# Four batches of normalised attention on one core: group statistics batch by batch, and the small step behind each row maximum on another engine

## The chip, the core and the metric

The kernel runs on one core of a Trainium2 chip. The metric is the device time of one execution in microseconds (us), taken as the median of several runs. The engines are named as in the profile: PE (TensorE, matrix products), PEld (its weight loads), DVE (VectorE), ACT (ScalarE), POOL (GpSimd) and SP (the queue that issues most transfers). They run their own instruction streams in order and wait for each other by semaphores.

## The reference

The input x has 4 batches of 128 channels and 32 x 32 = 1024 positions, all in float32. What is computed, for each batch:

```python
# 4 groups of 32 channels; mean and variance over a group's channels and all positions
y = (xg - mu) * rsqrt(var + 1e-5)
y = y * gamma + beta
q, k, v = split(w_qkv @ y + b_qkv)
w = softmax(q^T k * 128 ** -0.5)      # 1024 x 1024
out = x + w_out @ (v w^T) + b_out
```

## The kernel before

**Folding.** The products of the weight matrices are made once at the start. Scores come from z = (folded Wq, Wk) y and y itself, so a batch needs y, z and the values v (with the output matrix already in them). Most matrices are held as a head and a tail (names in _hi and _lo), and each product of them is three matmuls: hi by hi, hi by lo, lo by hi.

**Tiling.** A batch has 8 blocks of 128 query rows (i = 0 to 7), and each block has 1024 keys. "Block (b, i)" is block i of batch b. The steps of a block are:
- PE: scores of the block into PSUM, 128 x 1024 (block_scores, L601 to L604).
- DVE: negated row maximum (maximum, L427), then a small 128 x 1 operation that makes `shift` out of the maximum and the key bias of the row (L435).
- ACT: exponential with `shift` as bias, and the row sums (L276).
- DVE: reciprocal of the row sums, inv_sum (L440).
- POOL: probabilities times inv_sum (normalise, L216). "Normalisation" below is this.
- PE: eight 128 x 128 transposes (turn, L614), in two halves j = 0, 1.
- ACT and DVE: head and tail of the turned halves (pt_hi L285, pt_lo L447).
- PE: mixing with the values (mix, L634 to L636), a quarter of a half-batch at a time. The result of a half-batch is made on DVE (L454) and stored by SP.

**Order.** Every engine has its order written out by hand in a loop over b and i. In pass (b, i) PE makes the scores two blocks ahead, (b, i + 2), then turns block (b, i), then does a job of the next batch, then mixes. DVE takes the maximum of block i + 2, the tails of block i, a tail of a job, the result if one is due, then inv_sum of block i + 2. ACT makes the heads of block i and the exponential of block i + 2. POOL normalises block i + 2. Batch 0 has no mixing in its passes 0 to 3, since there is nothing to mix yet.

**Jobs of the next batch.** They project z in two halves (Z0, Z1) and the values in three parts (V0, V1, V2) into one PSUM bank, `projected`. JOB_SLOT puts Z0, V0, V1, Z1 into passes 4, 5, 6, 7 of the batch before; V2 comes in pass 0 of the batch itself. Each job waits until DVE has taken the tail of the one before (s_pj_lo, L567).

**Normalising x into y.** For batch 0 it is done in pieces at the start. For batch 1, POOL makes y in pass (0, 0) (L246) and its tail in passes (0, 2) and (0, 3) (y_tail, L211). For batches 2 and 3, DVE makes y in pass (b, 1) (L390), ACT its head in pass (b, 2), and POOL its tail in pass (b, 3) of the batch before.

**Statistics.** DVE: bn_stats of each half of x (L354, 128 x 512), bn_aggr to mean and variance of a channel (L359). PE: the deviation of each channel's mean from its group's, and the negated group mean (group_means, L547 and L549). DVE: spread (L367). PE: group variance (group_variances, L554). DVE: variance + eps (L372). POOL: power -0.5 (rstd_of, L204). DVE: norm_a, norm_b (coefficients, L378, L381). Batches 2 and 3 are done together: their four bn_stats stand in DVE's passes (0, 4) to (0, 7), group_means at the end of PE's pass (1, 0) behind a wait for the tail of V2 (L724), group_variances at the end of pass (1, 1), and the DVE and POOL steps in pass (1, 1).

Of the kernel before, what the change touches and what calls it, by code (L numbers as in the profile page):

```python
# [5 lines left out]
def attention_kernel(nc, x, vectors, weights, out):  # L6
# [4 lines left out]
    ALU = mybir.AluOpType  # L11
# [29 lines left out]
    with ctx:  # L41
# [33 lines left out]
        spread = sb("spread", [C, BATCHES])  # L75
        var_eps = sb("var_eps", [C, BATCHES])
        rstd = sb("rstd", [C, BATCHES])
        norm_a = sb("norm_a", [C, BATCHES])
        norm_b = sb("norm_b", [C, BATCHES])

# [18 lines left out]
        mixed = ps("mixed", [C, HALF])  # L99
        projected = ps("projected", [128, HALF])  # L100

        DEV, MINUS_MEAN, VARIANCE = 0, 8, 16
        setup = scores[:, 1, :]
        SET_W, SET_V, SET_OUT, SET_U, SET_S, SET_Z, SET_G = 0, 256, 384, 385, 386, 387, 512

# [8 lines left out]
        s_spread = sem("channel_spreads_ready")  # L114
        s_gvar = sem("group_variances_ready")
        s_var_eps = sem("variance_eps_ready")
        s_rstd = sem("rstd_ready")
        s_norm = sem("norm_ready")
        s_bias_product = sem("bias_product_ready")
# [66 lines left out]
        @block_ctx.gpsimd  # L186
        def _(pool):
            pool.memset(ident[:, :], 0.0).then_inc(s_const, 1)
            pool.memset(group_mean[:, :], 0.0).then_inc(s_const, 1)
            pool.memset(minus_half[:, :], -0.5).then_inc(s_const, 1)  # L190
            pool.memset(ones[:, :], 1.0).then_inc(s_const, 1)
            pool.wait_ge(s_const, 4)
            pool.affine_select(out=ident[:, :], in_=ident[:, :], compare_op=ALU.not_equal, fill=1.0,
                               base=0, pattern=[[-1, 128]], channel_multiplier=1).then_inc(s_const, 1)
            for g in range(GROUPS):
                pool.wait_ge(s_const, 5 + g)
                pool.memset(group_mean[g * CG:(g + 1) * CG, g * CG:(g + 1) * CG], 1.0 / CG).then_inc(s_const, 1)
            pool.wait_ge(s_const, 5 + GROUPS)
            pool.tensor_tensor(centring[:, :], ident[:, :], group_mean[:, :], ALU.subtract).then_inc(s_const, 1)
            pool.tensor_scalar(minus_mean[:, :], group_mean[:, :], -1.0, None, ALU.mult).then_inc(s_const, 1)  # L200

            def rstd_of(lo, hi, n):
                pool.wait_ge(s_var_eps, n)
                pool.tensor_tensor(rstd[:, lo:hi], var_eps[:, lo:hi], minus_half[:, lo:hi],  # L204
                                   ALU.pow).then_inc(s_rstd, 1)

            def y_tail(b, h):
                half = slice(h * HALF, (h + 1) * HALF)
                pool.wait_ge(s_y, b)
                pool.wait_ge(s_y_hi, b)  # L210
                pool.tensor_tensor(y_lo[:, b % 2, half], y[:, b % 2, half], y_hi[:, b % 2, half].bitcast(fp32),  # L211
                                   ALU.subtract).then_inc(s_y_lo, 1)

            def normalise(b, i):
                pool.wait_ge(s_inv, BLOCKS * b + i + 1)
                pool.tensor_scalar(probs[:, i % RING, :], probs[:, i % RING, :], inv_sum[:, i:i + 1], 1.0,  # L216
                                   ALU.mult, ALU.mult).then_inc(s_probs, 1)

            pool.wait_ge(s_vecs, 16)
            pool.tensor_tensor(bias_product[:, :], BQ, BK, ALU.mult).then_inc(s_bias_product, 1)  # L220
            rstd_of(0, 1, 1)
            rest = slice(SPLIT, N)
            pool.wait_ge(s_norm, 1)
            pool.tensor_scalar(y[:, 0, rest], xs[:, 0, rest], norm_a[:, 0:1], norm_b[:, 0:1],
                               ALU.mult, ALU.add).then_inc(s_y0_rest, 1)
            pool.wait_ge(s_y0_rest, 1)
            pool.wait_ge(s_y0_hi, 3)
            pool.tensor_tensor(y_lo[:, 0, rest], y[:, 0, rest], y_hi[:, 0, rest].bitcast(fp32),
                               ALU.subtract).then_inc(s_y0_lo_rest, 1)
            normalise(0, 0)  # L230
            rstd_of(1, 2, 2)
            normalise(0, 1)
            for b in range(BATCHES):
                for i in range(BLOCKS):
                    behind = 0 < b < BATCHES - 1 and i == 3
                    if behind:
                        y_tail(b + 1, 0)
                    if after(b, i, 2)[0] < BATCHES:
                        normalise(*after(b, i, 2))
                    if behind:  # L240
                        y_tail(b + 1, 1)
                    if b == 1 and i == 1:
                        rstd_of(2, BATCHES, 3)
                    if b == 0 and i == 0:
                        pool.wait_ge(s_norm, 2)
                        pool.tensor_scalar(y[:, 1, :], xs[:, 1, :], norm_a[:, 1:2], norm_b[:, 1:2],  # L246
                                           ALU.mult, ALU.add).then_inc(s_y, 1)
                    if b == 0 and i in (2, 3):
                        y_tail(1, i - 2)
# [95 lines left out]
        def _(dve):  # L345
# [29 lines left out]
            def coefficients(lo, hi, n, minus_means):  # L375
                dve.wait_ge(s_rstd, n)
                dve.wait_ge(s_gmean, 2 * n)
                step(dve.tensor_scalar(norm_a[:, lo:hi], rstd[:, lo:hi], GAMMA, None, ALU.mult))  # L378
                dve.wait_ge(s_step, steps_done[0])
                for b in range(lo, hi):  # L380
                    dve.scalar_tensor_tensor(out=norm_b[:, b:b + 1],  # L381
                                             in0=minus_means[:, MINUS_MEAN + b:MINUS_MEAN + b + 1],
                                             scalar=norm_a[:, b:b + 1], in1=BETA, op0=ALU.mult,
                                             op1=ALU.add).then_inc(s_norm, 1)

# [21 lines left out]
            def projection_tail(b, job):  # L407
                dve.wait_ge(s_pj_hi, job_count(b, job))
                if job in V_TILES:
                    key_biases(b, job, projected)  # L410
                    value_tails(b, job, projected, s_pj_lo)
                else:
                    half = slice(0, HALF) if job == Z0 else slice(HALF, N)
# [10 lines left out]
            def maximum(b, i):  # L424
                n = BLOCKS * b + i
                dve.wait_ge(s_scores, n + 1)
                dve.tensor_reduce(neg_max[:, i:i + 1], scores[:, i % 2, :], AX.X, ALU.max,  # L427
                                  negate=True).then_inc(s_max, 1)
                bias = key_bias[:, b % 2, i:i + 1]
                if n == 0:  # L430
                    dve.wait_ge(s_setup, 5)
                    first_key_biases(V0, turned[:, 1, :])
                dve.wait_ge(s_key_bias, 3 * b + min(i // 3, 2) + 1)
                dve.wait_ge(s_max, n + 1)
                dve.tensor_scalar(shift[:, i:i + 1], neg_max[:, i:i + 1], bias, bias, ALU.subtract,  # L435
                                  ALU.add).then_inc(s_shift, 1)

            def inverse_sum(b, i):
                dve.wait_ge(s_exp, BLOCKS * b + i + 1)
# [23 lines left out]
            variances(0, 1, 1, projected)  # L463
            half_stats(1, 0)
            dve.wait_ge(s_vecs, 16)
            coefficients(0, 1, 1, mixed)

            dve.wait_ge(s_norm, 1)
            pieces = (slice(0, FIRST), slice(FIRST, SPLIT))
# [35 lines left out]
            first_value_tails(V0, turned[:, 1, :])  # L505
            inverse_sum(0, 1)
            first_z_tail(3, projected[:, :], HALF, N)
            coefficients(1, 2, 2, mixed)

            for b in range(BATCHES):  # L510
                last = b + 1 == BATCHES
                for i in range(BLOCKS):
# [6 lines left out]
                    if b == 0 and i in (0, 1):  # L519
                        first_key_biases((V1, V2)[i], (mixed, projected)[i])  # L520
                        first_value_tails((V1, V2)[i], (mixed, projected)[i])
                    if b == 1 and i == 1:
                        channel_spreads(2, BATCHES, 6, projected)
                    if i in JOB_SLOT and not last:
                        projection_tail(b + 1, JOB_SLOT[i])
                    if i == 7:
# [2 lines left out]
                        results(b - 1, 1, mixed)  # L529
                    if ahead[0] < BATCHES:  # L530
                        inverse_sum(*ahead)
                    if b == 0 and i >= QB:
                        half_stats(2 + (i - QB) // 2, i % 2)
                        if i == 7:
                            channel_stats(2, BATCHES)
                    if b == 1 and i == 1:
                        variances(2, BATCHES, 3, projected)
                        coefficients(2, BATCHES, 3, projected)
                    if 0 < b and i == 1 and not last:
                        normalised(b + 1)  # L540
            results(BATCHES - 1, 1, projected)
# [2 lines left out]
        def _(pe):  # L544
# [17 lines left out]
                return mm  # L562

            def projection(b, job):
                if b == 2 and job == Z0:
                    pe.wait_ge(s_norm, BATCHES)
                if job_count(b, job) > 1:  # L567
                    pe.wait_ge(s_pj_lo, job_count(b, job) - 1)
                if job in V_TILES:
                    pe.wait_ge(s_y, b)  # L570
                    if b == 1 and job == V0:
                        pe.wait_ge(s_v0_lo, 3)
                    mm = values(b, job, projected)
                else:
                    half = slice(0, HALF) if job == Z0 else slice(HALF, N)
# [124 lines left out]
            for b in range(BATCHES):  # L700
                last = b + 1 == BATCHES
                for i in range(BLOCKS):
# [17 lines left out]
                        mix(b, 0, i - QB, mixed)  # L720
                    elif b > 0:
                        mix(b - 1, 1, i, mixed)
                    if b == 1 and i == 0:
                        pe.wait_ge(s_pj_lo, job_count(1, V2))  # L724
                        group_means(2, BATCHES, projected, projected)
                    if b == 1 and i == 1:
                        group_variances(2, BATCHES, projected)
            for chunk in range(QB):
                mix(BATCHES - 1, 1, chunk, projected)

# [30 lines left out]
```

## Time and profile before

| what | value |
|---|---|
| median of 3 runs | 153.50 us (153.49 to 153.58) |
| the profiled execution's own time | 153.87 us |
| its span (first to last instruction) | 152.1 us |
| PE busy | 143.5 us, 94% of the span |
| DVE busy | 117.5 us, 77% |
| ACT busy | 89.2 us, 59% |
| POOL busy | 51.3 us, 34% |
| granted PE clock | 1.00 |

The profile is of one execution. Its time is 1.77 us more than its span, and 0.37 us above the median of the runs. Times in the rows count from the start of the span. In a timeline row, the first number is the start of a group of instructions and the second the time from there to its end; where an instruction follows another on DVE or PE without a wait, it starts a little before the end of the first, since they are pipelined, so start-to-start distances are what an instruction costs its engine.

### The profile page before, as it was taken

The numbers are of one execution on the slowest core, as the hardware profiler recorded it, in microseconds if no ns is written. First come the engines' busy times: TensorE is split into PE (matmuls) and PEld (weight loads), VectorE is DVE, ScalarE is ACT, GpSimd is POOL, SyncE is SP. The second block draws the span as 40 slices with busy tenths as digits, with TensorE's granted clock in tenths as the row PEclk, the third lists the DMA queues.
The fourth block names the chain that finished last, engine by engine and source line by source line (L and its number), as shares of the span: only waits on it lengthen the run. The fifth ranks groups of instructions, "written<-read, shape, count | busy, mean of one in ns | idle before, by whom it ended". The sixth has DMA issues, their size and how long they took to land.

```text
span 152.1 us, 2244 instructions
## 1 busy us (share of the span) xinstructions
PE 143.5 (94%) x791; PEld 118.3 (78%) x791; DVE 117.5 (77%) x235; ACT 89.2 (59%) x163; POOL 51.3 (34%) x60
## 2 busy tenths in 40 slices
PE   7999999889999698999999999999999999999991
PEld 7977686578888577788888888888888888887880
DVE  0697799999889755997788979797779777977501
ACT  3164787896555543676677656866555666667200
POOL 6131517582222214176212224662221323232000
PEclk9999999999999999999999999999999999999999
DMA  5930000000000100001000200010000100010011
GB/s 176 312 134 0 0 4 0 2 0 0 4 2 18 51 0 0 0 23 50 0 0 0 73 0 2 0 71 0 4 0 3 66 0 0 10 66 0 0 69 69
DMA packets 2316, 4.60 MB, mean 30 GB/s; under 512 B 385, under 2 KB 385, under 8 KB 2305
## 3 DMA queue, kind: packets, MB, share of 16 engines
q1 hardware_dynamic: 2016, 4.20, 7.8%
q10 hardware_dynamic: 288, 0.27, 0.5%
q8 instruction: 6, 0.10, 0.3%
q14 instruction: 6, 0.04, 0.1%
HBM read 2.36 MB, written 2.10 MB: 29 GB/s over the span
## 4 chain that ended last, share of the span: by engine, by line
PE 80%; DVE 15%; ACT 2%; issue 1%; DVEq 0%
PE turned L614 15%; PE scores L601 8%; PE mixed L636 8%; PE scores L604 8%; PE mixed L635 8%; PE scores L602 8%; PE mixed L634 8%; DVE neg_max L427 5%; DVE pt_lo L447 4%; PE scores L641 4%; PE projected L560 3%; ACT probs L276 2%; DVE shift L435 1%; PE projected L636 1%; PE projected L635 1%
## 5 line engine op out<-in xcount | busy, mean ns | idle before, releaser
L216 POOL TENSOR_SCALAR probs<-probs,inv_sum 128x1024 f32<-128x1024 f32 x32 | 36.4, 1138 | 82.1 <-DVE inv_sum L440 82.1
L285 ACT ACTIVATE pt_hi<-turned 128x512 fp32r<-128x512 f32 x64 | 34.9, 595 | 39.1 <-PE turned L614 39.0
L427 DVE TENSOR_REDUCE neg_max<-scores 128x1 f32<-128x1024 f32 x32 | 39.0, 1218 | 12.8 <-PE scores L604 12.2
L447 DVE TENSOR_TENSOR pt_lo<-turned,pt_hi 128x512 fp32r<-128x512 f32 x64 | 40.9, 681 | 1.7 <-ACT pt_hi L285 1.7
L276 ACT ACTIVATE probs<-scores,shift 128x1024 f32<-128x1024 f32 x32 | 35.7, 1115 | 4.8 <-DVE shift L435 3.7
L614 PEld LDWEIGHTS turned<-ident,probs 128*128 128x128 f32 x256 | 29.3, 140 | 8.7 <-issue 3.5
L614 PE MATMUL turned<-ident,probs 128*128 128x128 f32 x256 | 34.0, 275 | 1.9 <-DVE pt_lo L447 1.5
L601 PE MATMUL scores<-y_hi,z_hi 128*128 128x512 f32 x62 | 24.9, 402 | 0.0
L602 PE MATMUL scores<-y_lo,z_hi 128*128 128x512 f32 x62 | 24.5, 395 | 0.0
L634 PE MATMUL mixed<-pt_hi,v_hi 128*128 128x512 f32 x56 | 23.9, 427 | 0.0
L636 PE MATMUL mixed<-pt_hi,v_lo 128*128 128x512 f32 x56 | 22.1, 395 | 0.0
L635 PE MATMUL mixed<-pt_lo,v_hi 128*128 128x512 f32 x56 | 22.1, 394 | 0.0
L604 PE MATMUL scores<-y_hi,z_lo 128*128 128x512 f32 x62 | 19.4, 394 | 0.0
L601 PEld LDWEIGHTS scores<-y_hi,z_hi 128*128 128x128 f32 x62 | 11.7, 188 | 2.7 <-issue 0.4
L604 PEld LDWEIGHTS scores<-y_hi,z_lo 128*128 128x128 f32 x62 | 11.6, 188 | 2.7
L602 PEld LDWEIGHTS scores<-y_lo,z_hi 128*128 128x128 f32 x62 | 11.7, 188 | 2.5
L636 PEld LDWEIGHTS mixed<-pt_hi,v_lo 128*128 128x128 f32 x56 | 10.5, 187 | 2.5
L635 PEld LDWEIGHTS mixed<-pt_lo,v_hi 128*128 128x128 f32 x56 | 10.6, 189 | 1.6
L634 PEld LDWEIGHTS mixed<-pt_hi,v_hi 128*128 128x128 f32 x56 | 10.6, 189 | 1.6
L435 DVE TENSOR_SCALAR shift<-neg_max,key_bias 128x1 f32<-128x1 f32 x32 | 8.7, 273 | 3.4
L211 POOL TENSOR_TENSOR y_lo<-y,y_hi 128x512 fp32r<-128x512 f32 x6 | 7.8, 1296 | 0.0
L354 DVE BATCH_NORM_STATS2 stats<-xs 128x6 f32<-128x512 f32 x8 | 5.4, 680 | 2.9 <-DMA xs<-in_x_dram 2.9
(142 smaller groups left out, 139.8 us busy)
## 6 DMA issues: line engine op xcount, KB each, us to landing
out_dram<-result SPq DMA_DIRECT2D x8, 256.0 KB, 2.1
xs<-in_x_dram SPq DMA_DIRECT2D x2, 512.0 KB, 6.7
xs<-in_x_dram SPq DMA_DIRECT2D x3, 256.0 KB, 4.6
xs<-in_x_dram ACTq DMA_DIRECT2D x1, 256.0 KB, 3.3
ws<-in_weights_dram SPq DMA_DIRECT2D x1, 256.0 KB, 4.4
vecs<-in_vectors_dram ACTq DMA_DIRECT2D x1, 3.0 KB, 4.6
```

Source lines behind the costliest of these rows:

```text
L216: pool.tensor_scalar(probs[:, i % RING, :], probs[:, i % RING, :], inv_sum[:, i:i + 1], 1.0, ALU.mult, ALU.mult).then_inc(s_probs, 1)
L276: act.activation(probs[:, i % RING, :], scores[:, i % 2, :], ACT.Exp, bias=shift[:, i:i + 1], accum_out=row_sum[:, i:i + 1]).then_inc(s_ex ...
L285: act.activation(pt_hi[:, g, j * 4:(j + 1) * 4, i % QB * 128:(i % QB + 1) * 128], turned[:, j, :].rearrange("p (k n) -> p k n", n=128), AC ...
L427: dve.tensor_reduce(neg_max[:, i:i + 1], scores[:, i % 2, :], AX.X, ALU.max, negate=True).then_inc(s_max, 1)
L447: dve.tensor_tensor(pt_lo[to], turned[:, j, :].rearrange("p (k n) -> p k n", n=128), pt_hi[to].bitcast(fp32), ALU.subtract).then_inc(s_pt_ ...
L601: pe.matmul(to[h], z_hi[:, b % 2, query], y_hi[:, b % 2, halves[h]], start=True, stop=False)
L602: pe.matmul(to[h], z_hi[:, b % 2, query], y_lo[:, b % 2, halves[h]], start=False, stop=False)
L604: mm = pe.matmul(to[h], z_lo[:, b % 2, query], y_hi[:, b % 2, halves[h]], start=False, stop=True)
L614: mm = pe.transpose(turned[:, j, k * 128:(k + 1) * 128], probs[:, i % RING, key:key + 128], ident[:, :])
L634: pe.matmul(bank[:, :], v_hi[v], pt_hi[:, g, k, :], start=(k == 0), stop=False)
L635: pe.matmul(bank[:, :], v_hi[v], pt_lo[:, g, k, :], start=False, stop=False)
L636: mm = pe.matmul(bank[:, :], v_lo[v], pt_hi[:, g, k, :], start=False, stop=(k == KT - 1))
```

## The change

Two edits, made together.

1. The operation that makes `shift` leaves DVE's stream (behind each maximum) and is issued by POOL instead. In pass (b, i) POOL makes `shift` of block i + 2 first, before its normalisation of the same block; the y and y_lo operations that POOL has in batch 0 stay behind the normalisation of their pass, and so stand in front of the next pass's `shift`. For blocks (0, 0) and (0, 1) POOL makes both shifts before the first normalisation.
2. The statistics of batches 2 and 3 are separate. Batch 2's bn_stats stand in DVE's passes (0, 4), (0, 5), batch 3's in (1, 4), (1, 5). group_means of batch b + 1 is issued just before the values of job V1 of batch b, group_variances just before those of job V2, in the same PSUM bank beyond the columns of the values (columns 400, 408, 416). DVE makes spread and a copy of the negated mean inside the tail of V1, and variance + eps inside that of V2. POOL makes rstd in pass (b, 0) behind the normalisation. The two waits at the end of PE's passes (1, 0) and (1, 1), and the wait before Z0 of batch 2, are gone.

```diff
-        DEV, MINUS_MEAN, VARIANCE = 0, 8, 16
+        DEV, MINUS_MEAN, VARIANCE = 400, 408, 416
...
@@ POOL
+            def shifts(b, i):
+                n = BLOCKS * b + i
+                bias = key_bias[:, b % 2, i:i + 1]
+                pool.wait_ge(s_key_bias, 3 * b + min(i // 3, 2) + 1)
+                pool.wait_ge(s_max, n + 1)
+                pool.tensor_scalar(shift[:, i:i + 1], neg_max[:, i:i + 1], bias, bias, ALU.subtract,
+                                   ALU.add).then_inc(s_shift, 1)
...
+            shifts(0, 0)
+            shifts(0, 1)
             normalise(0, 0)
             rstd_of(1, 2, 2)
             normalise(0, 1)
             for b in range(BATCHES):
                 for i in range(BLOCKS):
+                    if after(b, i, 2)[0] < BATCHES:
+                        shifts(*after(b, i, 2))
                     behind = 0 < b < BATCHES - 1 and i == 3
                     if behind:
                         y_tail(b + 1, 0)
...
-                    if b == 1 and i == 1:
-                        rstd_of(2, BATCHES, 3)
+                    if 0 < b < BATCHES - 1 and i == 0:
+                        rstd_of(b + 1, b + 2, b + 2)
@@ DVE, projection_tail
                     key_biases(b, job, projected)
+                    if job == V1 and b + 1 < BATCHES:
+                        channel_spreads(b + 1, b + 2, 2 * (b + 2), projected)
+                        dve.tensor_copy(negated_mean[:, b + 1:b + 2],
+                                        projected[:, MINUS_MEAN + b + 1:MINUS_MEAN + b + 2]).then_inc(s_negated, 1)
+                    if job == V2 and b + 1 < BATCHES:
+                        variances(b + 1, b + 2, b + 2, projected)
                     value_tails(b, job, projected, s_pj_lo)
@@ DVE, maximum
-                dve.wait_ge(s_key_bias, 3 * b + min(i // 3, 2) + 1)
-                dve.wait_ge(s_max, n + 1)
-                dve.tensor_scalar(shift[:, i:i + 1], neg_max[:, i:i + 1], bias, bias, ALU.subtract,
-                                  ALU.add).then_inc(s_shift, 1)
@@ DVE, loop
-                    if b == 1 and i == 1:
-                        channel_spreads(2, BATCHES, 6, projected)
...
-                    if b == 0 and i >= QB:
-                        half_stats(2 + (i - QB) // 2, i % 2)
-                        if i == 7:
-                            channel_stats(2, BATCHES)
-                    if b == 1 and i == 1:
-                        variances(2, BATCHES, 3, projected)
-                        coefficients(2, BATCHES, 3, projected)
+                    if b + 2 < BATCHES and i in (4, 5):
+                        half_stats(b + 2, i - 4)
+                        if i == 5:
+                            channel_stats(b + 2, b + 3)
+                    if 0 < b < BATCHES - 1 and i == 1:
+                        dve.wait_ge(s_negated, b)
+                        coefficients(b + 1, b + 2, b + 2, negated_mean[:, b + 1:b + 2])
@@ PE, projection
-                if b == 2 and job == Z0:
-                    pe.wait_ge(s_norm, BATCHES)
...
+                    if job == V1 and b + 1 < BATCHES:
+                        group_means(b + 1, b + 2, projected, projected)
+                    if job == V2 and b + 1 < BATCHES:
+                        group_variances(b + 1, b + 2, projected)
                     mm = values(b, job, projected)
@@ PE, loop
-                    if b == 1 and i == 0:
-                        pe.wait_ge(s_pj_lo, job_count(1, V2))
-                        group_means(2, BATCHES, projected, projected)
-                    if b == 1 and i == 1:
-                        group_variances(2, BATCHES, projected)
```

## Rows read from the trace of the kernel before

**Rows 1.** The page, part 1: busy time, share of the span and instructions.

```profile
PE 143.5 (94%) x791; PEld 118.3 (78%) x791; DVE 117.5 (77%) x235; ACT 89.2 (59%) x163; POOL 51.3 (34%) x60
```

**Rows 2.** Windows of PE alone: stretch, length, busy (instructions), clock, DMA, GB/s.

```profile
51.14:53.00 1.86, 0.64 (x6) 1.00 0.00 0
...
56.74:58.03 1.29, 0.41 (x3) 1.00 0.00 0
58.03:137.85 79.82, 79.82 (x445) 1.00 0.05 18
```

**Rows 3.** Timeline of PE: start, length, instruction, idle before and its releaser.

```profile
52.53 0.38 PE L547 MATMUL projected<-mean_var,centring 128*128 128x2 f32 x2 [1.22 <-DVE v_lo L404]
...
57.79 0.38 PE L554 MATMUL projected<-spread,group_mean 128*128 128x2 f32 x2 [0.88 <-DVE spread L367]
```

**Rows 4.** Timeline of DVE: passes (0, 0), (0, 1), and the end of (0, 5).

```profile
19.04 1.21 DVE L427 TENSOR_REDUCE neg_max<-scores 128x1 f32<-128x1024 f32 x1
...
20.55 1.28 DVE L447 TENSOR_TENSOR pt_lo<-turned,pt_hi 128x512 fp32r<-128x512 f32 x2
...
22.34 0.15 DVE L440 RECIPROCAL inv_sum<-row_sum 128x1 f32<-128x1 f32 x1
22.41 1.20 DVE L427 TENSOR_REDUCE neg_max<-scores 128x1 f32<-128x1024 f32 x1
...
38.90 0.15 DVE L440 RECIPROCAL inv_sum<-row_sum 128x1 f32<-128x1 f32 x1
38.97 0.67 DVE L354 BATCH_NORM_STATS2 stats<-xs 128x6 f32<-128x512 f32 x1
```

**Rows 5.** Timeline of POOL: passes (0, 0) and (0, 2).

```profile
22.58 1.12 POOL L216 TENSOR_SCALAR probs<-probs,inv_sum 128x1024 f32<-128x1024 f32 x1 [3.07 <-DVE inv_sum L440]
23.69 1.19 POOL L246 TENSOR_SCALAR y<-xs,norm_a,norm_b 128x1024 f32<-128x1024 f32 x1
...
29.85 1.29 POOL L211 TENSOR_TENSOR y_lo<-y,y_hi 128x512 fp32r<-128x512 f32 x1
```

**Rows 6.** Chain that ended last, pass (0, 2): from shift to inv_sum.

```profile
26.95 0.28 DVE shift L435
...
27.25 1.22 ACT probs L276 x2
```

**Rows 7.** Groups of instructions of POOL by form: busy, mean ns of one, idle before.

```profile
L246 POOL TENSOR_SCALAR y<-xs,norm_a,norm_b 128x1024 f32<-128x1024 f32 x1 | 1.2, 1193 | 0.0
L204 POOL TENSOR_TENSOR rstd<-var_eps,minus_half 128x1 f32<-128x1 f32 x2 | 1.1, 563 | 1.2 <-DVE var_eps L372 1.2
...
L224 POOL TENSOR_SCALAR y<-xs,norm_a,norm_b 128x384 f32<-128x384 f32 x1 | 0.7, 721 | 0.7 <-DVE norm_b L381 0.7
L204 POOL TENSOR_TENSOR rstd<-var_eps,minus_half 128x2 f32<-128x2 f32 x1 | 0.7, 712 | 0.0
L200 POOL TENSOR_SCALAR minus_mean<-group_mean 128x128 f32<-128x128 f32 x1 | 0.5, 535 | 0.0
...
L220 POOL TENSOR_TENSOR bias_product<-vecs 128x1 f32<-128x1 f32 x1 | 0.2, 194 | 2.3 <-DMA vecs<-in_vectors_dram 2.3
```

**Rows 8.** Timeline of PE: group_means of batch 1, and job V1 in pass (0, 6).

```profile
12.28 0.28 PE L547 MATMUL mixed<-mean_var,centring 128*128 128x1 f32 x2
...
12.64 0.92 PE L560 MATMUL turned<-wv_out,y 128*128 128x129 f32 x6
...
40.59 0.83 PE L560 MATMUL projected<-wv_out,y 128*128 128x129 f32 x6
```

**Rows 9.** Timeline of PE: turned blocks (1, 2) and (3, 6), then (3, 7).

```profile
63.32 1.17 PE L614 MATMUL turned<-ident,probs 128*128 128x128 f32 x8
...
138.36 1.16 PE L614 MATMUL turned<-ident,probs 128*128 128x128 f32 x8
...
140.77 1.04 PE L614 MATMUL turned<-ident,probs 128*128 128x128 f32 x8
```

**Rows 10.** Waits: who waited for whom, us in total, times, longest.

```profile
DVE neg_max L427 <- PE scores L604: 12.2, 17, 2.1
```

More of the change, by code:

```diff
@@ L77, in attention_kernel @@
         rstd = sb("rstd", [C, BATCHES])
+        negated_mean = sb("negated_mean", [C, BATCHES])
         norm_a = sb("norm_a", [C, BATCHES])
@@ L116, in attention_kernel @@
         s_var_eps = sem("variance_eps_ready")
+        s_negated = sem("negated_mean_kept")
         s_rstd = sem("rstd_ready")
@@ L380, in coefficients @@
                 for b in range(lo, hi):
-                    dve.scalar_tensor_tensor(out=norm_b[:, b:b + 1],
-                                             in0=minus_means[:, MINUS_MEAN + b:MINUS_MEAN + b + 1],
+                    dve.scalar_tensor_tensor(out=norm_b[:, b:b + 1], in0=minus_means[:, b - lo:b - lo + 1],
                                              scalar=norm_a[:, b:b + 1], in1=BETA, op0=ALU.mult,
@@ L428, in maximum @@
                                   negate=True).then_inc(s_max, 1)
-                bias = key_bias[:, b % 2, i:i + 1]
                 if n == 0:
@@ L465, in _ @@
             dve.wait_ge(s_vecs, 16)
-            coefficients(0, 1, 1, mixed)
+            coefficients(0, 1, 1, mixed[:, MINUS_MEAN:MINUS_MEAN + 1])
             dve.wait_ge(s_norm, 1)
@@ L507, in _ @@
             first_z_tail(3, projected[:, :], HALF, N)
-            coefficients(1, 2, 2, mixed)
+            coefficients(1, 2, 2, mixed[:, MINUS_MEAN + 1:MINUS_MEAN + 2])
             for b in range(BATCHES):
```

## The prediction

> **What bounds the kernel now.** Read the busy shares first: PE has 94% of the span, its clock is granted in full, and DVE has 77% [rows 1]. So only what keeps PE waiting, or gives it more to do, can move the end. I then cut PE's timeline into windows at its waits. From 58.03 to 137.85 us it is busy without a break [rows 2]: nothing taken off DVE, ACT or POOL there is worth anything while the rest still arrives in time. The waits stand earlier. (a) In passes (0, 0) to (0, 3), where nothing is mixed, PE follows DVE, and the chain of waits runs through maximum, shift, tails and inv_sum. (b) From 51.14 to 53.00 and from 56.74 to 58.03 PE stands before, and then does, the statistics matmuls of batches 2 and 3 [rows 2]; the releasers are DVE's v_lo and spread [rows 3]. Everything after 58.03 follows these two without slack, up to the last result.
>
> **Statistics: what goes.** With the waits gone, PE would go on with the next scores at 51.14 and 56.74. So 1.86 + 1.29 = 3.15 us leave the path, of which the matmuls are 0.47 (52.53 to 53.00) and 0.24 (57.79 to 58.03) [rows 2, 3]. What is late next? The scores of block (1, 3) need only the exponential of (1, 1), and the turn behind them needs DVE's tail of block (1, 0), which loses two bn_stats and two bn_aggr ahead of it (0.67 each, and less for the others) as well as a shift. I expect no new wait there.
>
> **What comes.** Per batch, group_means with one column costs PE 12.64 - 12.28 = 0.36 [rows 8] and group_variances about 0.25, taken at the 0.24 of the two-column one [rows 3]. Twice that, all on PE's path: 1.22. DVE gets two copies, one more variance, one more norm_a, each near 0.2, and bn_stats of batch 3 in passes (1, 4) and (1, 5). I cost these at nothing: DVE waits for PE's scores 17 times, 12.2 us in all [rows 10]. Without that cover they would be 0.8 and 1.6. POOL's rstd moves one pass ahead, behind normalisation (b, 2), and is wanted only after DVE's maximum and tails of the next pass. No DMA moves; the removed wait before Z0 of batch 2 held nothing.
>
> **Shift: what DVE saves.** From maximum to tails DVE needs 20.55 - 19.04 = 1.51 [rows 4]. A maximum with no dependent behind it holds DVE 1.14 (its 1.21, less the 0.07 by which 22.41 follows 22.34 + 0.15 = 22.49). So 0.37 less per block. In the PE-bound stretch that is worth nothing, except where DVE's tail held back the second half of a turn: blocks (1, 2) and (3, 6) take 1.17 and 1.16 where an unhindered one takes 1.04, and each also began late, about 0.27 in all for each [rows 9]. These go: 0.54.
>
> **Shift: what the new place costs.** The trace has no 128 x 1 POOL operation with two pointer operands. The y operations have that form: 1193 ns for 1024 columns, 721 for 384, so 0.74 ns a column and 0.44 us for none; the 128-column one of 535 ns lies on the same line [rows 7]. Bounds: 0.19 us, the one-column product, below; 0.71, the two-column power, above [rows 7]. I take s = 0.44, by the rows of the same operation. [...]
>
> The longer step alone would be hidden. What counts is POOL's order. Shift of the next block stands behind y (1.19) in pass (0, 0) and behind y_lo (1.29) in passes (0, 2) and (0, 3), and these start 1.11 after their normalisation [rows 5]. The chain in batch 0, from one inv_sum to the next, is then as follows.
> - inv_sum to normalisation 0.24 (22.34 to 22.58), to y 1.11, y 1.16: shift starts 2.51 after inv_sum [rows 4, 5]. Then s, 0.04 to ACT, 1.24 from exponential to inv_sum (27.25, with 1.22) [rows 6]: 3.79 + s = 4.23.
> - Behind y_lo: 0.10 more, 4.33.
> - With a free POOL: 0.07 to the maximum, 1.21, 0.09 to POOL, then the same: 2.65 + s = 3.09.
>
> Start: the maximum of (0, 2) at 19.04 [rows 4], moved by 0.07 for the shift before it. Shift 20.41, exponential 20.89, inv_sum (0, 2) at 22.13 (before, 22.34). Then (0, 3) behind y, 26.36; (0, 4), 29.45; (0, 5) behind y_lo, 33.78; (0, 6) behind y_lo, 38.11. DVE goes on: 0.07 and 0.60 for bn_stats, maximum 1.14, then the 1.79 that lie between 20.55 and 22.34 [rows 4] for tails, key_bias and v_lo: inv_sum (0, 7) at 41.71, where it was at 38.90 [rows 4]. Behind it come bn_stats (0.07 later, 0.67 [rows 4]) and a bn_aggr, for which I estimate 0.24, as for any small operation behind a wait on DVE; together 0.98, and only then may PE begin group_means, at about 42.8. It began V1 at 40.59 [rows 8]. So PE loses 2.2 us in batch 0; part of it is lost by pass (0, 4) already. The edits meet here: with either alone PE would not stand behind both POOL's queue and the new statistics. Behind that point the passes are mixed ones, longer than the chain, and no y work is on POOL.
>
> In batches 1 and 2 y_lo holds up the shift of block 6 too, by some 1.4 us. Its cover is the two-block lead: by the same steps bn_aggr of batch 3 ends about 0.5 us before PE wants it in pass (1, 6). I cost it at nothing.
>
> **Sum**, against the profiled execution: 153.87 - 3.15 - 0.54 + 1.22 + 2.2 = 153.6. The median of the runs stands 0.37 below that execution, so 153.2 is my forecast for it.
>
> **Rivals.**
> 1. The small operation is cheap (0.19). Five of them lie in the chain (blocks 2 to 6), one of them limited by DVE: 1.2 less, 152.0. For it: the product [rows 7]. Against it: the line of the y rows.
> 2. Slower: it is dear, as the power is (0.56 for one column, 0.71 for two [rows 7]), or takes as much longer to be noticed by ACT. Place: the same five steps in front of group_means in pass (0, 6). Five times 0.12 gives 153.8, five times 0.27 gives 154.5. It decides from about 0.50 on, where the whole gain is used up.
> 3. POOL's order doesn't bite: PE reaches V1 as before, because the exponentials have slack that I don't see. Then 153.50 - 3.15 - 0.54 + 1.22 = 151.0. Against it: the chain of waits runs through shift in these passes. What DVE saves there can't show, since inv_sum waits for the exponential.
> 4. The statistics of batch 3 come too late in pass (1, 6): each 0.1 beyond the 0.5 of cover costs 0.1, some 0.5 in all with the forecast's other terms, 153.7.
>
> **Chances.** Forecast 0.42, rival 1 0.20, rival 2 0.20, rival 3 0.08, rival 4 0.10. The range 151.9 to 154.4 leaves out rival 3 and the far end of rival 2. No change is within 0.2%, 0.3 us, about what a measurement of this kernel can tell. The forecast lies at its edge: I split it 0.22 faster, 0.15 same, 0.05 slower. Rivals 1 and 3 add 0.28 to faster, rivals 2 and 4 give 0.22 to slower and 0.08 to same. Faster 0.50, same 0.23, slower 0.27.
>
> **What would show it.** Right: shift of POOL near 440 ns; that of block (0, 3) starting right behind y, those of (0, 5) and (0, 6) right behind y_lo; inv_sum (0, 6) near 38; PE idle before group_means at about 41.5 to 42.8; the stretches of 1.86 and 1.29 gone; PE without a break from there on. Wrong: shift far from 440 ns, no idle time of PE before group_means in pass (0, 6), or a new wait of PE after 45 us.

## The result, and the profile after

The changed kernel takes 154.62 us (median of 6 runs, 154.37 to 154.87), the kernel before 153.53 (median of 6, 153.44 to 153.79): a ratio of 1.0069, 95% interval 1.0056 to 1.0083. It is slower; the forecast was 153.2 us and a range up to 154.4. Ratios here leave out a run that stands more than 1.5% above the fastest of its kernel: one of 6 of the kernel with POOL's order below (154.34) and one of 12 of the changed kernel with the other norm_b (156.63).

| what | before | after |
|---|---|---|
| the profiled execution's own time | 153.87 us | 154.79 us |
| its span | 152.1 us | 153.0 us |
| PE busy | 143.5 us | 144.6 us |
| DVE busy | 117.5 us | 112.2 us |
| POOL busy | 51.3 us | 62.7 us |

The page of the changed kernel, parts 1 and 5, against [rows 1] and [rows 7] (an engine's busy time; then line, operation, count, busy us, mean ns, idle before it and its releaser):

```profile
PE 144.6 (95%) x797; PEld 120.0 (78%) x797; DVE 112.2 (73%) x207; ACT 89.0 (58%) x163; POOL 62.7 (41%) x93
...
L226 POOL TENSOR_SCALAR shift<-neg_max,key_bias 128x1 f32<-128x1 f32 x32 | 11.7, 366 | 25.1 <-DVE neg_max L446 22.2
```

DVE has 5.3 us less to do, POOL 11.4 us more; the 32 shifts are 11.7. Neither is the bound. What counts is which of them PE waits for. POOL's timeline after, from pass (0, 0) to pass (0, 4), answers to [rows 5]:

```profile
22.86 1.13 POOL L218 TENSOR_SCALAR probs<-probs,inv_sum 128x1024 f32<-128x1024 f32 x1 [1.54 <-DVE inv_sum L454]
23.97 1.19 POOL L260 TENSOR_SCALAR y<-xs,norm_a,norm_b 128x1024 f32<-128x1024 f32 x1
25.15 0.36 POOL L226 TENSOR_SCALAR shift<-neg_max,key_bias 128x1 f32<-128x1 f32 x1
27.04 1.12 POOL L218 TENSOR_SCALAR probs<-probs,inv_sum 128x1024 f32<-128x1024 f32 x1 [1.53 <-DVE inv_sum L454]
28.23 0.36 POOL L226 TENSOR_SCALAR shift<-neg_max,key_bias 128x1 f32<-128x1 f32 x1
30.13 1.12 POOL L218 TENSOR_SCALAR probs<-probs,inv_sum 128x1024 f32<-128x1024 f32 x1 [1.53 <-DVE inv_sum L454]
31.22 1.27 POOL L213 TENSOR_TENSOR y_lo<-y,y_hi 128x512 fp32r<-128x512 f32 x1
32.48 0.37 POOL L226 TENSOR_SCALAR shift<-neg_max,key_bias 128x1 f32<-128x1 f32 x1
34.38 1.11 POOL L218 TENSOR_SCALAR probs<-probs,inv_sum 128x1024 f32<-128x1024 f32 x1 [1.53 <-DVE inv_sum L454]
35.46 1.29 POOL L213 TENSOR_TENSOR y_lo<-y,y_hi 128x512 fp32r<-128x512 f32 x1
36.73 0.37 POOL L226 TENSOR_SCALAR shift<-neg_max,key_bias 128x1 f32<-128x1 f32 x1
```

Three of these four shifts stand behind a normalisation and y or y_lo, the one at 28.23 behind a normalisation alone; after each shift POOL idles 1.53 us. DVE's timeline of the changed kernel shows who waits for the exponential behind that shift, and where the statistics of batch 2 end, against [rows 4]:

```profile
26.78 0.16 DVE L454 RECIPROCAL inv_sum<-row_sum 128x1 f32<-128x1 f32 x1 [1.24 <-ACT probs L290]
...
34.12 0.16 DVE L454 RECIPROCAL inv_sum<-row_sum 128x1 f32<-128x1 f32 x1 [1.53 <-ACT probs L290]
...
38.37 0.16 DVE L454 RECIPROCAL inv_sum<-row_sum 128x1 f32<-128x1 f32 x1 [1.11 <-ACT probs L290]
...
42.06 0.16 DVE L454 RECIPROCAL inv_sum<-row_sum 128x1 f32<-128x1 f32 x1
...
42.84 0.21 DVE L373 BATCH_NORM_AGGREGATE mean_var<-stats 128x2 f32<-128x12 f32 x1
```

DVE stands still for 1.24, 1.53 and 1.11 us. PE's timeline of the changed kernel, from the turn in pass (0, 6) on, against [rows 8] (V1 began at 40.59):

```profile
40.99 1.16 PE L628 MATMUL turned<-ident,probs 128*128 128x128 f32 x8
43.20 0.35 PE L559 MATMUL projected<-mean_var,centring 128*128 128x1 f32 x2 [1.04 <-DVE mean_var L373]
43.42 0.36 PE L561 MATMUL projected<-mean_var,minus_mean 128*128 128x1 f32 x2
43.64 0.92 PE L572 MATMUL projected<-wv_out,y 128*128 128x129 f32 x6
```

**Where the time went.** The turns (eight transposes a block, one group in PE's timeline) serve as milestones. In both kernels all up to group_means of batch 1 on PE is the same, and it came 0.45 later in the changed kernel's trace (12.73, before 12.28 [rows 8]); that is taken off here. Distances are after minus before.

| PE begins | after - before, less 0.45 | what happened since the row above |
|---|---|---|
| turn (0, 4) | +0.78 | shift of block (0, 3) behind y |
| turn (0, 6) | +0.82 | shift of block (0, 5) behind y_lo, covered by mixing |
| turn (0, 7) | +2.68 | PE waits for bn_aggr of batch 2, then group_means |
| turn (1, 1) | +0.95 | the old wait of 1.86 is gone |
| turn (1, 2) | -0.41 | the old wait of 1.29 is gone |
| turn (1, 3) | -0.20 | held back itself, for pt_lo of block (1, 2) |
| turn (1, 7) | +0.39 | group_means of batch 3, and a short wait |
| turn (2, 1) | +0.60 | group_variances of batch 3 |
| turn (2, 4) | +0.74 | turn (2, 3) held back, for pt_lo of block (2, 2) |
| turn (3, 6) | +0.44 | nothing holds it back any more |
| last result | +0.48 | |

One name has to be put right first. The row at 63.32 in [rows 9] is the turn of block (1, 3), not (1, 2) as its heading and the prediction say, and some expectations below repeat it: it waits for pt_lo of block (1, 2). In the changed kernel the same turn has a wait that PE's timeline shows:

```profile
63.57 1.16 PE L628 MATMUL turned<-ident,probs 128*128 128x128 f32 x8 [0.21 <-DVE pt_lo L461]
```

From group_means of batch 1 to the last result the kernel before takes 136.57 us (12.28 to 148.85) and the changed one 137.05 (12.73 to 149.78). I call this the body; its end is the start of the last result on DVE. A second trace of the kernel before gave the same 136.57, and no other kernel was traced twice: two traces that agree are the ground for comparing bodies to a few hundredths, more closely than the medians.

### The profile page after: what moved, and what is told of

Same layout as the page of the kernel before. It is cut to its first block, busy times and chain, and to the rows that moved or that the text cites. A ratio compares the mean times of both kernels' runs of the same rounds, so it can differ in the third digit from the quotient of the medians.

```text
span 153.0 us, 2261 instructions
## 1 busy us (share of the span) xinstructions
PE 144.6 (95%) x797; PEld 120.0 (78%) x797; DVE 112.2 (73%) x207; ACT 89.0 (58%) x163; POOL 62.7 (41%) x93
## 4 chain that ended last, share of the span: by engine, by line
PE 74%; DVE 10%; POOL 6%; ACT 4%; issue 3%; POOLq 0%
PE turned L628 14%; PE mixed L650 7%; PE mixed L648 7%; PE mixed L649 7%; PE scores L616 7%; PE scores L618 7%; PE scores L615 7%; DVE neg_max L446 5%; ACT probs L290 4%; PE scores L655 4%; PE projected L572 3%; POOL probs L218 2%; POOL shift L226 2%; POOL y_lo L213 2%; PE projected L650 1%
## 5 line engine op out<-in xcount | busy, mean ns | idle before, releaser
L218 POOL TENSOR_SCALAR probs<-probs,inv_sum 128x1024 f32<-128x1024 f32 x32 | 35.8, 1119 | 46.4 <-DVE inv_sum L454 46.4
L226 POOL TENSOR_SCALAR shift<-neg_max,key_bias 128x1 f32<-128x1 f32 x32 | 11.7, 366 | 25.1 <-DVE neg_max L446 22.2
L454 DVE RECIPROCAL inv_sum<-row_sum 128x1 f32<-128x1 f32 x32 | 5.2, 162 | 14.0 <-ACT probs L290 13.4
L572 PE MATMUL projected<-wv_out,y 128*128 128x129 f32 x52 | 7.8, 281 | 0.0
```

## Experiments

**The kernel before, traced again.** No edit.

> The kernel before once more, for a second trace of it. Expected: 153.5 us, the 1.86 and 1.29 us waits again. Open: whether the first matmuls behind the warm-up run at the short or the long spacing, and where the profiled execution of 153.87 us lost 0.37 us against the median.

Measured: 153.62 us, span 151.8, body 136.57, batch 1's group_means at 12.03. The waits stand as before. So the 0.37 us of the first trace don't lie in the body; 0.25 of them lie ahead of 12.28.

**Each edit alone.** First the statistics, with shift in DVE's stream again:

```diff
@@ POOL, shifts
                 n = BLOCKS * b + i
+                if not (False):
+                    return
...
@@ DVE, maximum
+                if True:
+                    bias = key_bias[:, b % 2, i:i + 1]
+                    dve.wait_ge(s_key_bias, 3 * b + min(i // 3, 2) + 1)
+                    dve.wait_ge(s_max, n + 1)
+                    dve.tensor_scalar(shift[:, i:i + 1], neg_max[:, i:i + 1], bias, bias, ALU.subtract,
+                                      ALU.add).then_inc(s_shift, 1)
```

> Edit 2 alone; shift is made by DVE again. Theory (the statistics pay 1.9 us, the place of shift in POOL's order takes them back): the waits of 1.86 and 1.29 us are gone, 1.2 us of small matmuls come, PE doesn't wait before group_means in pass (0, 6); 151.6 to 151.9 us. Rival (the statistics matmuls inside the value jobs are what costs): 153.5 us or more, with PE idle before group_means in pass (0, 6).

Measured: 152.15 us, ratio 0.9887 (0.9867 to 0.9906), body 135.05, 1.52 less than before. bn_aggr of batch 2 is done well ahead of PE:

```profile
39.81 0.21 DVE L375 BATCH_NORM_AGGREGATE mean_var<-stats 128x2 f32<-128x12 f32 x1
```

```profile
40.73 0.28 PE L567 MATMUL projected<-mean_var,centring 128*128 128x1 f32 x2
40.87 0.36 PE L569 MATMUL projected<-mean_var,minus_mean 128*128 128x1 f32 x2
41.09 0.92 PE L580 MATMUL projected<-wv_out,y 128*128 128x129 f32 x6
```

The first fence is DVE's timeline, the second PE's, both of this kernel: no releaser stands behind L567. The expected 151.6 to 151.9 was missed by 0.25, for which the run with the other norm_b, below, has the cause. Then shift on POOL in the kernel before, with the statistics untouched (shifts as in the change, and DVE's own operation gone):

```diff
...
+            shifts(0, 0)
+            shifts(0, 1)
             normalise(0, 0)
...
+                    if after(b, i, 2)[0] < BATCHES:
+                        shifts(*after(b, i, 2))
...
```

> Edit 1 alone; the statistics of batches 2 and 3 as before. Theory: inv_sum of blocks (0, 3), (0, 5), (0, 6) late as in the changed kernel, PE 1.2 us late by pass (0, 4) and more by pass (0, 6), where it waits for v_lo; the two old waits stand but are shorter, as DVE has less to do: 153.7 to 154.8 us. Rival (the move of shift is free, the two edits only collide at group_means): within 0.3 us of 153.5.

Measured: 154.09 us beside 154.10 of the kernel before in the same runs, 1.0013 (0.9996 to 1.0029); the time decides nothing, the trace does. inv_sum of (0, 3), (0, 5), (0, 6) came late behind y and y_lo, and PE was 1.19 us late at turn (0, 7) and 0.42 in the body. PE's waits in this kernel (us in total, times, longest), against the 1.22 and 0.88 of [rows 3]:

```profile
PE projected L554 <- DVE v_lo L416: 1.0, 1, 1.0
...
PE projected L561 <- DVE spread L379: 0.5, 1, 0.5
```

So the move of shift costs 1.2 us in batch 0 and is paid back in part by the two old waits, which shrink since DVE has less to do. Together with edit 2 nothing is left to shrink, and a new wait stands in front of group_means. The parts don't add: -1.52 and +0.42 alone, +0.48 together.

**POOL's order.** Both edits, but y and the y_lo operations stand behind the shift of the next pass and ahead of its normalisation:

```diff
                     if after(b, i, 2)[0] < BATCHES:
                         shifts(*after(b, i, 2))
-                    behind = 0 < b < BATCHES - 1 and i == 3
-                    if behind:
-                        y_tail(b + 1, 0)
-                    if after(b, i, 2)[0] < BATCHES:
-                        normalise(*after(b, i, 2))
-                    if behind:
-                        y_tail(b + 1, 1)
-                    if 0 < b < BATCHES - 1 and i == 0:
-                        rstd_of(b + 1, b + 2, b + 2)
-                    if b == 0 and i == 0:
+                    if b == 0 and i == 1:
                         pool.wait_ge(s_norm, 2)
                         pool.tensor_scalar(y[:, 1, :], xs[:, 1, :], norm_a[:, 1:2], norm_b[:, 1:2],
                                            ALU.mult, ALU.add).then_inc(s_y, 1)
-                    if b == 0 and i in (2, 3):
-                        y_tail(1, i - 2)
+                    if b == 0 and i in (3, 4):
+                        y_tail(1, i - 3)
+                    if 0 < b < BATCHES - 1 and i in (3, 4):
+                        y_tail(b + 1, i - 3)
+                    if after(b, i, 2)[0] < BATCHES:
+                        normalise(*after(b, i, 2))
+                    if 0 < b < BATCHES - 1 and i == 0:
+                        rstd_of(b + 1, b + 2, b + 2)
```

> Both edits, but POOL's y and y_lo operations stand behind the next block's shift and ahead of its normalisation, where POOL was idle. Theory (the order of POOL's queue): shifts start within 0.2 us of their maximum, inv_sum (0, 6) before 36.5, no wait of PE before group_means in pass (0, 6) beyond 0.3 us: 151.6 to 152.4 us. Rival (the longer operation and the second handover by themselves): PE's loss in batch 0 remains at 1.5 us or more, above 153.5 us.

Measured: 151.87 us, ratio 0.9853 (0.9827 to 0.988), body 134.42, 2.63 less than the changed kernel's. POOL's timeline in this kernel:

```profile
22.97 1.13 POOL L218 TENSOR_SCALAR probs<-probs,inv_sum 128x1024 f32<-128x1024 f32 x1 [1.53 <-DVE inv_sum L451]
24.17 0.36 POOL L226 TENSOR_SCALAR shift<-neg_max,key_bias 128x1 f32<-128x1 f32 x1
24.51 1.19 POOL L251 TENSOR_SCALAR y<-xs,norm_a,norm_b 128x1024 f32<-128x1024 f32 x1
26.07 1.12 POOL L218 TENSOR_SCALAR probs<-probs,inv_sum 128x1024 f32<-128x1024 f32 x1 [0.36 <-DVE inv_sum L451]
```

y now lies in the 1.53 us in which POOL had been idle, and delays nobody: inv_sum (0, 6) starts at 35.11, bn_aggr at 39.81. The instructions, their lengths and the handover are the same as in the changed kernel, so the rival (the longer operation by itself) falls.

**Only y moved.** As above for y alone; the y_lo operations stay.

> The changed kernel with only y of batch 1 moved behind the shift of block (0, 3); the y_lo operations stay where the change has them. Theory (each of the three y operations delays the chain by its own length): inv_sum (0, 3) 1.1 us earlier, PE at group_means 1.1 us earlier, 153.4 to 153.6 us. Rival (y_lo are enough to make PE late, y is hidden): 154.3 us or more.

Measured: 153.27 us, ratio 0.9966 (0.9946 to 0.9986), body 136.07, 0.98 less than the changed kernel's. From batch 1's group_means to those of batch 2 it takes 29.44 (12.34 to 41.78), in the changed kernel 30.47 (12.73 to 43.20) and with all three operations moved 28.05 (12.82 to 40.87). So of 2.42, y alone makes 1.03 and the y_lo operations the rest. The time is 0.13 below the expected range, the 1.1 expected at group_means was 1.03.

**A second shift.** A useless copy in front of each of five shifts of batch 0:

```diff
+                if 2 <= n <= 6:
+                    pool.tensor_scalar(spare[:, i:i + 1], neg_max[:, i:i + 1], bias, bias, ALU.subtract,
+                                       ALU.add)
```

> The changed kernel with a second, useless copy of the shift operation on POOL in front of each of the shifts of blocks 2 to 6 of batch 0 (it writes a spare tile). Theory (all five lie in the chain in front of group_means in pass (0, 6)): five times about 0.35, group_means 1.6 to 1.8 us later than in the changed kernel, 156.2 to 156.4 us. Rival (only those behind y and y_lo are in the chain): three times 0.35, 155.6 us. If nothing is in the chain: 154.6.

Measured: 155.90 us, ratio 1.0135 (1.0111 to 1.016), body 138.55. Counted from batch 1's group_means (12.09 here), those of batch 2 start at 32.25, in the changed kernel at 43.20 - 12.73 = 30.47: 1.78 later, five times 0.36. All five stand in the chain: it is this distance that decides against the rival of three, since the time lies between the two forecasts. The body is 1.50 longer: 0.3 is given back where turn (1, 3) is held up less. The time came out 0.3 below the expected range.

**Shift on DVE in batch 0 only.** The changed kernel with the shifts of b = 0 in DVE's stream.

> The changed kernel with shift on DVE in batch 0 and on POOL in batches 1 to 3. Theory (only the five shifts of batch 0 in front of group_means are late on PE's path): 151.9 to 152.3 us, near edit 2 alone. Rival (shift on POOL costs in every batch): halfway, 153.3 us or more.

Measured: 152.22 us, ratio 0.9892 (0.9872 to 0.9912), body 134.85. The loss is in batch 0. But between turns (1, 6) and (1, 7) PE needs 5.30 us, in the statistics-alone kernel 4.78. PE's timeline of this kernel says why:

```profile
74.57 0.35 PE L567 MATMUL projected<-mean_var,centring 128*128 128x1 f32 x2 [0.28 <-DVE mean_var L375]
```

The 0.28 is counted from the end of the turn. From start to start, group_means begins 1.32 behind turn (1, 6) (73.25) and 0.88 in the statistics-alone kernel, and its first step is 0.08 longer: 0.52.

**And batch 3's bn_stats two passes earlier.** The kernel above with

```diff
-                    if b + 2 < BATCHES and i in (4, 5):
-                        half_stats(b + 2, i - 4)
-                        if i == 5:
+                    if b + 2 < BATCHES and i in ((4, 5) if b == 0 else (2, 3)):
+                        half_stats(b + 2, i % 2)
+                        if i % 2 == 1:
```

> The kernel with shift on DVE in batch 0 and on POOL behind it, with batch 3's bn_stats in DVE's passes (1, 2) and (1, 3) instead of (1, 4) and (1, 5). Theory (its PE waits about 0.5 us for bn_aggr of batch 3 in pass (1, 6), since POOL's y_lo holds back the shift of block (1, 6)): that wait goes, 151.6 to 151.8 us against 152.22. Rival (the loss there is something else): 152.2 us, the step between blocks (1, 6) and (1, 7) stays near 5.3 us.

Measured: 151.68 us, ratio 0.9867 (0.9842 to 0.9891), body 134.60. The step from (1, 6) to (1, 7) is 4.78 again. Turn (1, 4) is held up instead: the job behind it begins 1.05 after the turn's start, where it was 0.80. So the body gains 0.25, not 0.5.

**norm_b with one tensor operand.** In the changed kernel norm_b of batches 2 and 3 reads the kept negated mean and BETA as tensors in SBUF, where it read the mean from PSUM before. DVE's timeline in pass (1, 1) of the changed kernel, and POOL's beside it:

```profile
59.57 0.21 DVE L392 TENSOR_SCALAR norm_a<-rstd,vecs 128x1 f32<-128x1 f32 x1
59.82 1.02 DVE L395 SCALAR_TENSOR_TENSOR norm_b<-negated_mean,norm_a,vecs 128x1 f32<-128x1 f32 x1
60.88 0.81 DVE L403 TENSOR_SCALAR y<-xs,norm_a,norm_b 128x1024 f32<-128x1024 f32 x1
```

```profile
59.72 1.12 POOL L218 TENSOR_SCALAR probs<-probs,inv_sum 128x1024 f32<-128x1024 f32 x1 [1.53 <-DVE inv_sum L454]
```

A 128 x 1 operation takes 1.02 us and ends at 60.84, when POOL's normalisation ends (59.72 + 1.12). The same instruction for batch 1 reads its mean from PSUM, also while POOL normalises. Its row, and POOL's beside it, both of the changed kernel:

```profile
19.44 0.22 DVE L395 SCALAR_TENSOR_TENSOR norm_b<-mixed,norm_a,vecs 128x1 f32<-128x1 f32 x1
```

```profile
18.82 1.12 POOL L218 TENSOR_SCALAR probs<-probs,inv_sum 128x1024 f32<-128x1024 f32 x1
```

POOL is busy until 19.94, and norm_b takes 0.22. So it is the second operand in SBUF that makes the difference. The edit:

```diff
-                    dve.scalar_tensor_tensor(out=norm_b[:, b:b + 1], in0=minus_means[:, b - lo:b - lo + 1],
-                                             scalar=norm_a[:, b:b + 1], in1=BETA, op0=ALU.mult,
-                                             op1=ALU.add).then_inc(s_norm, 1)
+                    dve.tensor_scalar(norm_b[:, b:b + 1], minus_means[:, b - lo:b - lo + 1],
+                                      norm_a[:, b:b + 1], BETA, ALU.mult, ALU.add).then_inc(s_norm, 1)
```

> The changed kernel with norm_b as a tensor_scalar: one tensor operand (the kept negated mean) and two pointer operands, in place of a scalar_tensor_tensor with two tensor operands in SBUF. Theory (that DVE instruction waits for POOL's normalisation, 59.82 to 60.84, because of its second SBUF tensor operand): norm_b of batches 2 and 3 takes 0.2 to 0.3 us, and PE's losses at blocks (1, 2) and (2, 3) go, 0.3 to 0.5 us less than the changed kernel's 154.6. Rival (it takes long because of the wait for norm_a, or of the copy in SBUF): still near 1.0 us, and no gain.

Measured: 154.01 us (the kernel before beside it 153.86, 1.0007, 0.9992 to 1.0022), body 136.72, 0.33 less than the changed kernel's. Turn (2, 3) is no longer held up, turn (1, 3) still is a little (1.16). DVE's timeline now:

```profile
59.65 0.28 DVE L395 TENSOR_SCALAR norm_b<-negated_mean,norm_a,vecs 128x1 f32<-128x1 f32 x1
59.96 1.26 DVE L402 TENSOR_SCALAR y<-xs,norm_a,norm_b 128x1024 f32<-128x1024 f32 x1
```

norm_b is short, but y behind it took 1.26 in place of 0.81, ending at 61.22; POOL's normalisation ran until 60.68. Of the 0.74 taken off norm_b, y gives 0.45 back.

**The same with POOL's y work behind the shift, and with the statistics alone.**

> Both edits with POOL's y work behind the next shift, and norm_b as a tensor_scalar. Theory: the two gains add, 151.3 to 151.6 us. Rival (the next limit stands at once, nothing added): 151.9 us.

Measured: 151.33 us, ratio 0.9837 (0.9819 to 0.9856), body 133.95. On top of the other order, the other norm_b takes another 0.47 off the body (134.42 - 133.95). This is the fastest version found, below both kernels.

> Edit 2 alone, shift on DVE, norm_b as a tensor_scalar. Theory: 0.3 to 0.5 us less than the 152.15 of edit 2 alone. It also says what the place of shift is worth once nothing stands in its way in POOL's queue: against the kernel with POOL's y work behind the shift, equal within 0.3 us if PE is the limit in both.

Measured: 151.90 us, ratio 0.987 (0.985 to 0.9889), body 134.49, 0.56 less than with the other norm_b, which is what edit 2 alone had missed. With a free POOL queue the move of shift is thus worth 134.49 - 133.95 = 0.54 us: 0.27 at turn (3, 6), most of the rest in batch 0. The expectation that the two would be equal within 0.3 was wrong.

## Why the prediction was wrong

**What held.** The mechanism, nearly to the tenth. Counted from batch 1's group_means, the prediction's inv_sum (0, 6) was at 25.83 (38.11 - 12.28), measured 25.64; its group_means of batch 2 at 30.5, measured 30.47. Up to turn (1, 2) its sum is -3.15 + 0.61 + 2.2 = -0.34, measured -0.41. That POOL's order is the cause, the runs show by moving it. The operation's length was 0.37, not 0.44, and the handover from maximum to POOL was 0.16 to 0.18 (at block (0, 2) the maximum ends at 20.78 and shift starts at 20.96) and not 0.09. Where shift follows the maximum directly the two misses cancel, by luck: 3.09 forecast for the step between inv_sums, 3.09 measured. Behind y and y_lo only the shorter operation counts: 4.18 and 4.25 measured, 4.23 and 4.33 forecast. The steps written down add up to 42.7 for group_means, and the "about 42.8" has 0.1 without a source; from the end of bn_aggr to group_means the trace has 0.15 (43.05 to 43.20). The second rival's 154.5 lies next to the measured time, but its cause is absent: the operation was cheaper than forecast, not dearer.

**What failed**, from the forecast's -0.27 to +0.48 in the body:
1. "These go: 0.54." At the end it did (0.30 at turn (3, 6)). At the row called block (1, 2), turn (1, 3), it didn't: where 0.27 was to be won, 0.21 were lost. The prediction counted norm_b as before, and it waits for POOL. A rule that the prediction left out stands in the Trainium skill (GPSIMD Engine Reference, section 1): POOL shares its SBUF interfaces with DVE, and DVE instructions with two SBUF inputs contend. The trace agrees: 1.02 us with two inputs in SBUF, 0.22 with one of them in PSUM, POOL running both times. The diff showed that norm_b's input moves from PSUM to SBUF; the prediction counted the copy and not the place. At turn (2, 3) 0.14 more went. Together 0.62. The run with the other norm_b took back 0.44 of them (0.30 up to turn (1, 3), 0.14 at turn (2, 3)); the other 0.18 remain at turn (1, 3), where y then takes 1.26, and no run separates them.
2. "group_means with one column costs PE 0.36." Behind a turn it costs 0.44 (4.78 for the step from (1, 6) to (1, 7) in the statistics-alone kernel, 4.34 before). 12.28 to 12.64 stood behind other matmuls.
3. "bn_aggr of batch 3 ends about 0.5 us before PE wants it." It was the fourth rival: PE waited 0.15. In the kernel with DVE's shifts in batch 0, where PE arrives earlier, 0.52. At turn (1, 3) PE was 0.20 earlier than in the kernel before. That the 0.5 was counted against PE's old times, and that POOL's y_lo had moved with DVE, is argued, not shown. Here the prediction's own sign of being wrong, a new wait of PE after 45 us, came true, as it did with the 0.21 at 63.57.

The second and the third concern batch 3. The three make 0.62 + 0.08 + 0.15 = 0.85; the early part (-0.07) and group_variances (-0.04) take some back, and the end adds 0.01: 0.75.

**What was not in the body.** "The median of the runs stands 0.37 below that execution." I carried that difference over to the changed kernel as if it were a constant. In its case the profiled execution (154.79) lies 0.17 above the median. So the miss of 1.39 us (154.62 against 153.23, the sum before rounding) is 0.75 in the body, 0.45 ahead of it and 0.20 in this step, to 0.01. The stretch ahead of batch 1's group_means, the same PE instructions in every kernel here, ended between 12.03 and 12.84 in 13 traces, and the kernel before itself gave 153.44 to 154.36 us over all runs, where three runs had shown 153.49 to 153.58. Beside the later medians of the kernel before (153.83 to 154.10), 154.62 would be 0.5 to 0.8 slower, near the body's 0.48; in the first comparison it was 1.09. Whether the rest is chance or a trait of the changed kernels' start, the runs don't settle.

## What to carry to other kernels

Look at what stands in the queue ahead of a small operation that many wait for. Here the large ones fitted where the queue was idle, between shift and normalisation, and the same edit turned from a loss into a gain. Moving an operand of a DVE instruction from PSUM to SBUF can change what it waits for, as it did for norm_b, so look at what POOL does at that moment. Before a second edit is counted beside the first, see whether both lean on the same slack.

## What the hardware showed beyond that

- **DVE and POOL in SBUF.** A 128 x 1 DVE instruction with two tensor operands in SBUF took 1.02 us both times (59.82 and 93.28), to the end of POOL's normalisation; with one of the two in PSUM 0.22, and with one tensor operand 0.27 to 0.28, POOL busy in each case. DVE's y (128 x 1024, one tensor operand) took 0.81 alone and 1.26 when POOL had begun first. Which property of y makes it wait, no run here separates.
- **PE's start.** After the same warm-up matmuls the next eight took 1.66 us in the changed kernel's trace (5.46 to 7.12) and 0.92 in the first trace of the kernel before (5.72 to 6.64), the first two of them spaced 0.22 and 0.14. PE's timelines, after first, then before:

```profile
5.46 0.42 PE L661 MATMUL scores<-ident,ws 128*128 128x128 f32 x1
5.68 0.42 PE L662 MATMUL scores<-ident,ws 128*128 128x128 f32 x1
```

```profile
5.72 0.30 PE L647 MATMUL scores<-ident,ws 128*128 128x128 f32 x1
5.86 0.27 PE L648 MATMUL scores<-ident,ws 128*128 128x128 f32 x1
```

The granted clock reads 1.00 in both. In the four traces with the short spacing (0.12 to 0.14) batch 1's group_means began at 12.03 to 12.28, in the nine with 0.21 or 0.22 at 12.34 to 12.84. Both traces of the kernel before are among the four, and two of the eleven others; why a start is of one kind or the other stays open. It moves the time by a few tenths of a microsecond, as much as the effect sought; a milestone behind it and a difference of bodies do better than medians.
